# One ScalarE change in a fused state-space and expert layer: gelus of two expert tiles in every second turn, and the expert normalisation moved from VectorE to ScalarE

## The reference, cut to what matters

```python
def mamba(x, ...):                       # x: 8 sequences of 1024 tokens, 256 channels, 16 states
    x_ssm, x_gate = split(x @ W_in + b_in)
    x_conv = silu(conv4(x_ssm) + conv_b)
    B, C = split(x_conv @ W_bc + b_bc);  dt = softplus(x_conv @ W_dt + b_dt)
    h[t] = h[t-1] * exp(dt[t] * A) + (dt[t] * x_conv[t]) * B[t]
    y[t] = sum_n(h[t] * C[t]) + x_conv[t] * D
    return layernorm((y * silu(x_gate)) @ W_out + b_out + x) * ln_g + ln_b
def ffn(x, ...):                         # 8 experts, top 2, hidden 512
    combine = top2(softmax(x @ gate_w))
    h = gelu(layernorm(x @ w1[e] + b1[e]) * ln1_g[e] + ln1_b[e])
    return layernorm(sum_e(combine[e] * (h @ w2[e] + b2[e])) + x) * ln_g + ln_b
xn = layernorm(x);  out = x + mamba(xn) + ffn(xn)
```

## Time and profile before

| | |
|---|---|
| median of 3 runs (lowest to highest) | 1819.2 us (1811.06 to 1820.54) |
| profiled execution: time, span | 1810.14 us, 1808.1 us |
| PE busy | 1546.5 us, 86% |
| DVE busy | 1534.0 us, 85% |
| ACT busy | 1458.1 us, 81% |
| POOL busy | 1009.1 us, 56% |
| granted TensorE clock in the main stage | 1.00 of full speed |

### The profile page before, as it was taken

One profiled execution on the slowest core, in us unless ns is written; L12 is line 12 of the kernel. 1 busy time (PEld: TensorE's weight loads), 2 busy tenths in 40 slices (PEclk: granted clock), 3 DMA queues, 4 the chain that ended last, 5 costly groups with the idle time before them and its releaser, 6 DMA issues.

```text
span 1808.1 us, 28219 instructions
## 1 busy us (share of the span) xinstructions
PE 1546.5 (86%) x6882; PEld 941.6 (52%) x6882; DVE 1534.0 (85%) x2498; ACT 1458.1 (81%) x2552; POOL 1009.1 (56%) x594
## 2 busy tenths in 40 slices
PE   5988379898988998989899888989888998886588
PEld 4655145555555565555555555555555655554232
DVE  5766488999999999999898989999999999931797
ACT  3554279898989889898989898989889898966587
POOL 2777756655655656555655556556556565532233
PEclk9777789999999999999999999999999999999799
DMA  7999643333334333333333433333333333322995
GB/s 234 351 294 377 238 119 84 95 97 99 95 84 112 84 95 90 100 90 100 83 103 86 109 84 102 98 92 98 89 103 84 94 97 95 88 45 48 284 293 175
DMA packets 183269, 234.43 MB, mean 130 GB/s; under 512 B 46527, under 2 KB 148936, under 8 KB 183131
## 3 DMA queue, kind: packets, MB, share of 16 engines
q1 hardware_dynamic: 141646, 171.58, 30.9%
q0 software_dynamic: 26160, 36.06, 10.7%
q10 hardware_dynamic: 15328, 25.20, 4.0%
HBM read 149.07 MB, written 83.70 MB: 129 GB/s over the span
## 4 chain that ended last, share of the span: by engine, by line
DVE 40%; ACT 26%; issue 14%; PE 13%; ACTq 3%; POOL 2%; DMA 1%; DVEq 0%; SPq 0%; POOLq 0%
DVE area L1285 8%; DVE area L1298 5%; ACT area L667 4%; DVE area L1315 4%; DVE area L1294 4%; ACT psD L661 3%; DVE more L1347 3%; ACT L706 3%; ACT h_T L701 3%; ACT L709 3%; PE psT L1030 3%; PE psX L982 3%; DVE h_norm L1328 2%; DVE more L1344 2%; ACTq L688 2%
## 5 line engine op out<-in xcount | busy, mean ns | idle before, releaser
L543 POOL TENSOR_TENSOR area<-area,more 128x1024 f32<-128x1024 f32 x258 | 604.4, 2360 | 547.5 <-DVE area L1298 276.3
L1315 DVE TENSOR_TENSOR area<-area,psD 128x1024 f32<-128x1024 f32 x256 | 310.0, 1211 | 0.3 <-issue 0.2
L972 PE MATMUL psH<-w_sb,ffn_xT 128*128 x544 | 265.0, 610 | 5.8 <-ACT ffn_xT L677 5.7
L520 POOL DMA_INDIRECT expert_d<-y_out,meta x139 | 219.6, 1580 | 78.4 <-ACT y_out L683 49.6
L982 PE MATMUL psX<-w_sb,h_T 128*128 x1088 | 261.6, 383 | 0.8 <-ACT y_out L683 0.8
L1003 PE MATMUL psY<-ident,area 128*128 128x128 f32 x2048 | 250.7, 276 | 0.0
L982 PEld LDWEIGHTS psX<-w_sb,h_T 128*128 128x128 f32 x1088 | 202.4, 190 | 59.4 <-issue 32.5
L667 ACT ACTIVATE area<-area,A_sb 128x512 f32<-128x512 f32 x258 | 171.5, 712 | 76.5 <-DVE area L1298 41.4
L1003 PEld LDWEIGHTS psY<-ident,area 128*128 128x128 f32 x2048 | 222.2, 141 | 13.4
L701 ACT ACTIVATE h_T<-psT,be_T,g_T 128x128 f32<-128x128 f32 x540 | 202.2, 460 | 4.5 <-PE psT L962 4.5
L661 ACT ACTIVATE psD<-area,A_sb 128x512 f32<-128x512 f32 x258 | 177.9, 690 | 33.9 <-DVE area L1285 14.5
(11 more groups left out here) (187 smaller groups left out, 2492.2 us busy)
## 6 DMA issues: line engine op xcount, KB each, us to landing
more<-B_rows_d SPq DMA_DIRECT2D x130, 512.0 KB, 3.9
xin<-sorted_x SPq DMA_DIRECT2D x137, 128.0 KB, 2.1
more<-ssm_d SPq DMA_DIRECT2D x18, 512.0 KB, 3.9
area<-xnT_d SPq DMA_DIRECT2D x17, 512.0 KB, 3.6
mamba_d<-mo_stage SPq DMA_DIRECT2D x17, 512.0 KB, 2.9
area<-L_attn_x SPq DMA_DIRECT2D x8, 1024.0 KB, 6.8
xnT_d<-w_sb ACTq DMA_DIRECT2D x16, 512.0 KB, 6.8
expert_d<-area ACTq DMA_DIRECT2D x8, 1024.0 KB
```

Of the source, the lines that this page charges most:

```text
L543: pool.tensor_tensor(inflow[:, k], dtx, B_rep[par][:, k].rearrange("p (a t) -> p a t", a=1).to_broadcast([P, KD, CHUNK]), ALU.mult).then_i ...
L972: nc.tensor.matmul(psH[:, :], ffn_xT[:, k, :], w1_sb[:, bass.ds(e, 1), k, :].rearrange("p o h -> p (o h)"), start=(k == 0), stop=False)
L1315: V.tensor_tensor(h, h, C_rep[k].rearrange("p (a t) -> p a t", a=1) .to_broadcast([P, KD, CHUNK]), ALU.mult).then_inc(S[f"hC{k}_done"], 1)
```

## The change

In every second turn ScalarE loads the gelu table once and does the gelus of two tiles, the previous turn's and this turn's. Its other turn needs no gelu table. The normalisation of the hidden values moves from DVE to ScalarE: DVE makes `neg_mean`, ScalarE multiplies it by the root (`hnm`) and applies both in one `Identity` activation over 128x512. In the turn without gelus the root, the normalisation and `copy_xT` come first, ahead of the three decay steps. A tile is projected down two turns after its own turn and copied out three turns after it (`LAG` 3), so `h_norm` gets a second and `h_T` a third buffer. Both silus of a chunk share one table load in turn 1. On TensorE the turned hidden values of an odd tile come at the end of its turn and those of an even tile behind `up` and `spread_C0` of its turn.

```diff
-LAG = 2
+LAG = 3
@@ ScalarE @@
+            def hidden_norm(u):
+                act.wait_ge(S["rstd_ready"], u + 1)
+                act.wait_ge(S["mean_ready"], u + 1)
+                nc.scalar.activation(hnm[:, :], neg_mean[:, :], ACT.Copy, scale=hrs[:, 0:1]).then_inc(S["shift_ready"], 1)
+                act.wait_ge(S["shift_ready"], u + 1)
+                if u >= 2:
+                    act.wait_ge(S["hT_done"], u - 1)
+                nc.scalar.activation(h_norms[u % 2], psH[:, :], ACT.Identity, scale=hrs[:, 0:1], bias=hnm[:, 0:1]
+                                     ).then_inc(S["norm_done"], 1)
+            def gelu(u):
+                e = expert(u)
+                act.wait_ge(S["hT_done"], u + 1)
+                if u >= 3:
+                    act.wait_ge(S["y_ready"], u - 2)
...
-                        e, e_y = expert(u), expert(u - LAG)
-                        decay0_of(u + 1, 0, state[0], g, par)
-                        decay1_of(u + 1, state[1], par)
-                        hidden_root(u)
...
+                        if pr % 2 == 1:
+                            hidden_root(u)
+                            hidden_norm(u)
+                            copy_xT(u + 1)
+                            decay0_of(u + 1, 0, state[0], g, par)
+                            decay1_of(u + 1, state[1], par)
+                            decay0_of(u + 1, 1, state[0], g, par)
+                            if u >= LAG:
+                                copy_y(u - LAG)
+                            if TASKS[pr - 1] is not None:
+                                take(TASKS[pr - 1], g, ahead)
+                        else:
+                            decay0_of(u + 1, 0, state[0], g, par)
+                            decay1_of(u + 1, state[1], par)
+                            hidden_root(u)
+                            hidden_norm(u)
...
+                            decay0_of(u + 1, 1, state[0], g, par)
+                            copy_xT(u + 1)
+                            if u >= LAG:
+                                copy_y(u - LAG)
+                            if pr == 0:
+                                copy_sum(c)
...
-                        with_gelu()
-                        copy_y(u, (pr - LAG) % RING, pr % 2, e_y)
-                        gelu(u, pr % 2, e)
+                        if pr % 2 == 0:
+                            with_gelu()
+                            if u > 0:
+                                gelu(u - 1)
+                            gelu(u)
+                            with_exp()
                         if pr == CONV_TURN:
+                            gate_silu_of(c, half)
                             act.wait_ge(S["seed_done"], g + 1)
                             conv_silu(g)
-                        if pr == GATE_TURN:
-                            gate_silu_of(c, half)
-                        with_exp()
+                            with_exp()
@@ TensorE, main turns @@
+                        if u == 0:
+                            wait_taken("gate1", 0)
+                            transpose_h(0)
+                        up(u + 1)
+                        spread_C0(u + 1, state[0], par, g)
+                        if pr % 2 == 0:
+                            if u > 0:
+                                transpose_h(u)
+                            transpose_x(u + 2)
+                            if pr == 0:
+                                transpose_sum(c)
+                            early_C = pr not in (CONV_TURN - 1, DT_TAKEN + 1)
+                            if early_C:
+                                spread_C1(u + 1, state[1], par)
+                            if u >= 2:
+                                down(u - 2)
...
+                            add_up(u, pr % 2)
+                            if TASKS[pr] is not None:
+                                pe.wait_ge(S["gelu_done"], u + 1)
+                                task(TASKS[pr], g)
+                        else:
...
+                            add_up(u, pr % 2)
+                            wait_taken(TASKS[pr], g)
+                            transpose_h(u)
@@ VectorE @@
+                if u > 0:
+                    dve.wait_ge(S["norm_done"], u)
                 V.bn_aggr(hmv[:, :], hstats[:, :]).then_inc(S["var_ready"], 1)
+                dve.wait_ge(S["var_ready"], u + 1)
+                V.tensor_scalar(neg_mean[:, :], hmv[:, 0:1], -1.0, None, ALU.mult).then_inc(S["mean_ready"], 1)
-                        hidden_norm(u)
-                        if pr == BC_TAKEN:
+                        if pr == BC_TAKEN + 1:
                             bc_residue(g, ahead)
```

More of the change, by code:

```diff
@@ L240, in build_program @@
         hrs = sb("hrs", [P, 1])
+        neg_mean = sb("neg_mean", [P, 1])
+        hnm = sb("hnm", [P, 1])
         tiles_of, tiles_end, skipped = (sb(f"te{i}", [P, EXPERTS]) for i in range(3))
@@ L824, in _ @@
             for u in range(MAMBA_TURNS, FFN_TURNS):
-                e, e_y = expert(u), expert(u - LAG)
                 copy_xT(u + 1)
                 hidden_root(u)
+                hidden_norm(u)
+                copy_y(u - LAG)
                 with_gelu()
-                copy_y(u, (u - LAG) % RING, u % 2, e_y)
-                gelu(u, u % 2, e)
+                if u == MAMBA_TURNS:
+                    gelu(u - 1)
+                gelu(u)
                 with_exp()
@@ L834, in _ @@
                         take_out(CHUNKS, j, psY[:, j * CHUNK:(j + 1) * CHUNK])
-            for u in range(FFN_TURNS, FFN_TURNS + LAG):
-                copy_y(u, (u - LAG) % RING, u % 2, expert(u - LAG))
+            for t in range(FFN_TURNS - LAG, FFN_TURNS):
+                copy_y(t)
             def root(k, off):
@@ L881, in _ @@
         def _(pe):
-            for name, ahead in (("tr_ready", 1), ("sum_done", 2), ("hT_done", 1)):
+            for name, ahead in (("tr_ready", 1), ("sum_done", 2)):
                 pe.sem_inc(S[name], ahead)
@@ L1076, in _ @@
             transpose_x(0)
-            for k in range(KD):
-                m = nc.tensor.transpose(psX[:, DIM + k * P:DIM + (k + 1) * P], ident[:, :], ident[:, :])
-            m.then_inc(S["y_ready"], 1)
             pe.wait_ge(S["w_ffn"], W_FFN)
             pe.wait_ge(S["b_rows_in"], 48)
-            up(0, expert(0))
+            up(0)
             transpose_x(1)
@@ L1110, in _ @@
-                        if pr == TASKS.index("out0"):
-                            project_out(c, 0, psT[:, :])
-                        elif pr == TASKS.index("out1"):
-                            project_out(c, 1, psT[:, :])
-                        elif TASKS[pr] is not None:
-                            task(TASKS[pr], g)
-                        if not early_C:
-                            transpose_x(u + 2)
-                            spread_C1(u + 1, state[1], par)
-                        down(u - 1, (pr + 1) % 2, e_down)
@@ new lines, in _ @@
+                            if not early_C:
+                                spread_C1(u + 1, state[1], par)
+                            if pr == 0:
+                                seed(c)
+                            add_up(u, pr % 2)
+                            if TASKS[pr] is not None:
+                                pe.wait_ge(S["gelu_done"], u + 1)
+                                task(TASKS[pr], g)
+                        else:
+                            early_C = pr != CONV_TURN
+                            if early_C:
+                                transpose_x(u + 2)
+                                spread_C1(u + 1, state[1], par)
+                            pe.wait_ge(S["gelu_done"], u)
+                            if TASKS[pr - 1] is not None:
+                                wait_taken(TASKS[pr - 1], g)
+                            if pr == TASKS.index("out0"):
+                                project_out(c, 0, psT[:, :])
+                            elif pr == TASKS.index("out1"):
+                                project_out(c, 1, psT[:, :])
+                            else:
+                                task(TASKS[pr], g)
+                            if not early_C:
+                                transpose_x(u + 2)
+                                spread_C1(u + 1, state[1], par)
+                            if u >= 2:
+                                down(u - 2)
+                            add_up(u, pr % 2)
+                            wait_taken(TASKS[pr], g)
+                            transpose_h(u)
@@ L1132, in _ @@
                 transpose_x(u + 2)
-                down(u - 1, (u - 1) % 2, e_down)
-            down(FFN_TURNS - 1, (FFN_TURNS - 1) % 2, expert(FFN_TURNS - 1))
+                down(u - 2)
+            for t in range(FFN_TURNS - 2, FFN_TURNS):
+                down(t)
             pe.wait_ge(S["mo_copied"], 2 * CHUNKS + 2)
@@ L1450, in _ @@
             gate(CHUNKS, 1)
-            with dve.Fori(MAMBA_TURNS, FFN_TURNS) as u:
+            for u in range(MAMBA_TURNS, FFN_TURNS):
                 hidden_stats(u)
```

(1 more changed line is left out.)

137 lines of the change are left out of this document (57 added, 80 removed).

## The result

The kernel became slower: 1869.5 us median of 4 runs (1863.24 to 1876.06) against 1816.8 (1811.06 to 1820.54), ratio 1.028, interval 1.0248 to 1.0311. The forecast was 1796, its range ended at 1828. The profiled execution has a span of 1866.8 us, before 1808.1: 58.7 more.

What follows compares the result with a forecast made beforehand. DVE bound most turns before and ACT some; after the change ACT would set the pace. Profiled 1810.1 - 28 (main stage) + 5 (tail) = 1787, so 1796 against the median; range of 8 in 10: 1774 to 1828.

Steps and rivals of the forecast that it cites:

- Part 2: ACT's operations through a pair of turns: 18.8 us where DVE needs 15.4, so ACT sets the pace.
- B: Pair of turns 3 and 4 of a chunk: 18.7 us, before 19.7.
- C: Pair of turns 5 and 6 of a chunk: 19.4 us, before 19.4.
- Part 3: Lengths of a chunk's four pairs of turns: -1.5 us a chunk, -2.0 in the other half, -28 in sixteen chunks.
- A: Pair of turns 1 and 2: DVE stays the bound, 25.3 us, before 25.7.
- D: Pair of turns 7 and 0: set by ACT's walk, 20.5 us, before 20.7.
- The wait ahead of the gate: In A, DVE's gate waits for TensorE's turn of the sums, queued behind gelus: 0.7 us (bounds 0 and 1.5).
- down by about 70 us: Sign that the forecast is right: DVE's busy time in the whole kernel falls by about 70 us.
- Part 4: The last seven tiles: a turn takes 7.4 us, before 6.8; +5 us in all (0 to +10).
- Rival 1: DVE stays the bound everywhere and each turn gains 0.5 us: 1757 us; chance 6%.
- Rival 2: 0.5 us more in each of B, C and D, from semaphore latencies or a costlier `hnm`: 1810 to 1828; chance 18%.
- Rival 3: ACT's reads of the expert number lie exposed: one a pair costs 26 us, two give 1848; chance 16%.

Runs made afterwards that it cites:

- Experiment 3: Changed kernel with the spread of C ahead of the second product on TensorE in turn 6: 1866.9 us, ratio 1.028.
- Experiment 6: Changed kernel with GpSimd's second inflow of each turn on half its elements: 1837.7 us, ratio 1.009.
- experiment 1: Changed kernel with the hidden normalisation back on VectorE, gelus still paired: 1803.4 us, ratio 0.992.
- v3: Kernel of experiment 1; in the last seven turns root and table load ahead of the tile copy, transpositions ahead of the first product: 1787.5 us, ratio 0.985.
- e10: Changed kernel; in the last seven turns only, normalisation on VectorE beside the table load and transpositions ahead of the first product: 1863.1 us, ratio 1.026.
- v4: v3 with the convolution's first head between the scans of turn 0 and its second ahead of the gate in turn 1: 1778.6 us, ratio 0.980.

## Why the prediction was wrong, point by point

- **Part 2, ACT's walk**: right in mechanism for B and C, and nearly in size. B was forecast at 18.6 and lasted 19.3, C at 19.3 and lasted 20.0: 22 us in 16 chunks. `hnm` and the normalisation are 0.1 longer each than I took, twice a pair: 0.4 of the 0.7. The rule that the prediction weighed, the Trainium skill, "ScalarE: Activation LUTs", "What ACT_TABLE_LOAD costs" (93 ns a pointer operand), agrees: 0.78 for the normalisation, 0.68 for the take. Its drain of 1.38 us is in neither trace: 1.30 from the load's start to the first gelu's.
- **Part 3, A and D**: the step that failed, and the largest miss. A and D were forecast at 45.6 and lasted 48.3: 2.7 x 16 = 43 us.

  In A, I took DVE's saving of 1.44 less 0.4 as time off the pair. The two taps beside GpSimd took 0.95 of it back, and DVE is busy 25.05 there, before 24.94. The wait ahead of the gate was 0.68, as forecast (0.7).

  D, I took as set by ACT's walk. In D of after DVE waits for no decay at all. It is busy 20.7, before 19.3: L1420 is 1.4 longer, and the lowest part of B and C (L1415, 1.04 in the mean) has moved from turn 5 to turn 7, for which the prediction had no term. And it waits 1.0 for the spread of C (1.5 in the chunk shown), behind a product that ran at the lower clock in 10 of 16 chunks. I had written that DVE would want the spread when it came, and did not ask at what clock PE would do the product ahead of it.

  In the same way I counted the end of the wait of the earlier trace rows as pure gain. The term for DVE's busy time, "down by about 70 us", came out at +5.

  Experiment 3 shows that the losses of D stand behind one another: take away one, and the other remains. Experiment 6 takes 1.7 of the 2.7 away with shorter inflows. How much each carries alone stays open.
- **The granted clock** was 1.00 before and 0.96 in the main stage after. PE now stands for the gelus 1.5 us in turn 0, 1.7 in turn 6 and about 0.6 in turns 2 and 4; that this lowers the clock is likely, but no run parts it from the rest. The prediction had no term for it. Between after and experiment 1 the clock is nearly the same (0.96 and 0.97) and the time 66 us apart, so it is not the main cause.
- **Part 4, the tail**: +5 (0 to +10), measured +20. From the last second scan to the last statistics it lost 11.6 us, and from there to the last scatter 8.6, of which the third tile of the lag is about 4.5. I had ACT's own work at 6.2 and a turn at 7.4; a turn took 8.5 to 9.7. Of the 20 us, 7 go when the normalisation is back on DVE (experiment 1: 91.7), and the other 13 when root and table load stand ahead of the tile copy and the transpositions ahead of the first product (v3: 78.7). The kernel before had 78.8 with the tile copy first, so that order is no part of what the change cost. The order of before, with the normalisation on DVE in the tail (e10), gave 92.4. What took these 13, apart from about 4.5 for the third tile, stays open. Before, ACT loaded the gelu's table beside DVE's normalisation; now both are ACT's, and PE waits 3.0 us for the normalisation ahead of the first product, which was at the lower clock for some of its time in six of seven turns:

```profile
1691.93 0.78 ACT L710 ACTIVATE h_norm<-psH,hnm,hrs 128x512 f32<-128x512 f32 x1
```

```profile
1692.95 3.49 PE L1012 MATMUL psH<-w_sb,ffn_xT 128*128 x4 [3.01 <-ACT h_norm L710]
```

- **Rival 1** (DVE the bound): wrong here, right in experiment 1. Its product 128 x 0.5 is 64 and not 67, which changes nothing. **Rival 2** (0.5 more in B, C and D): B and C did this, with 0.7 each, but D had 1.7, by another cause. **Rival 3** (exposed reads of the expert number): not seen; the copy of y starts 0.26 after the tile copy does (705.90 and 706.16), without a gap.
- What the prediction never asked: what the kernel would do with the normalisation left on DVE. The walk of part 2 had DVE 3 us idle in each pair and ACT without a gap but the one between the gelus, and the change moves 0.58 + 0.22 a turn onto ACT (measured 0.68 + 0.33). That was in its own numbers: 108 us of ACT time bought 64 of DVE's, which DVE did not need.

The version that the runs point to is v4: normalisation on VectorE, gelus paired, taps ahead of the second scan, and in the tail the root and the transpositions first. It takes 1778.6 us: 2.0% under before and 4.9% under the changed kernel.

## What to carry to other kernels

When a change frees one engine and loads another, work out which of the two has the idle time after the change, and price both halves of the change apart: here one half was worth -14 us and the other +66. An operation that is moved forward in time meets other neighbours, also when it moves because a wait ahead of it is gone. Look at what the other engines do in the new place, and take its length from a row with that neighbour. A gap on an engine is only free as long as what it does next is not late.

## What the runs showed of the hardware

- A DVE operation whose operands all lie in SBUF and that starts beside GpSimd's product of two SBUF tiles ends only 0.27 to 1.09 us after it, the longer ones later, in 62 of 62 cases of three lines: 0.54 became up to 1.98 (the tap), 1.22 became 2.45 to 2.79 (L1420), and in experiment 3 0.68 became 2.16 (L1415). DVE's products with an operand in PSUM kept 1.22 beside the same inflow.
- GpSimd's scatter took 2.38 us instead of 1.58 in 15 turns of after, in which it ran beside the end of L1420 and the operation behind it (L1424). Before, 14 scatters that ran beside the first of these two alone kept 1.57.
- Behind a wait of PE of 1.72 us in turn 6 the same eight matmuls took 3.2 to 3.6 us in 10 of 16 chunks of after, at a granted clock of 0.54 to 0.60, and 1.99 in the other 6. In the tail four took 2.4 to 3.8 instead of 1.98 in six of seven turns. So a stretch at the lower of the two clocks often followed such a wait, but not always.
